# A decoder layer on one core: the last chunk's units as four heads by half the queries, and its first half's tail beside the last four units

## The chip, the cores and the metric

One core of a Trainium2 chip runs the kernel. Its engines are TensorE (PE, with a weight load of its own, PEld), VectorE (DVE), ScalarE (ACT), GpSimd (POOL) and SyncE (SP), which issues the DMAs here. Every engine works through its own queue in order and waits on semaphores. The metric is the device time of one launch in microseconds.

## The reference

Four sequences of 1024 tokens of width 256 pass a layer of three parts; each part reads the layer norm of what is so far and adds to it.

```python
h = layernorm(x)                                  # (4, 1024, 256)
q, k, v = split(h @ qkv_w.T + qkv_b)              # 16 query heads, 4 key/value heads of 64
q = q * (r / sqrt(64) * softplus(scaling))
x = x + softmax(q @ k.T) @ v @ o_w.T + o_b        # each key/value head serves 4 query heads
h = layernorm(x)                                  # cross-attention to 64 context rows, 16 heads of 16
x = x + softmax(mask(h @ Wq @ kc.T / 4)) @ vc @ Wout + bout
h = layernorm(x)                                  # routed feed-forward: 8 clusters of 8 tiles
tile = argmax over the gates of the best cluster
comp = tanh(gelu(h @ cw1) @ cw2)
mag = relu(comp @ w1[tile] + b1[tile]) @ w2[tile] + b2[tile]
x = x + layernorm(h + mag * directions[tile] * scale) * gamma + beta
```

## The kernel before

The tokens are 8 chunks of 512 (CHUNKS, two for a sequence). Attention runs in 64 units; a unit is two query heads of one key/value head over the 512 queries of a chunk, and has 8 steps (KT), one for each 128 keys. In a step PE makes the scores of both heads (`scores`: six matmuls, since q and k are kept as a high and a low part), ACT takes one exponential of 128x1024, PE multiplies the probabilities of two steps before with the values (`attend`), and DVE and POOL add them up for one head each (`add`). The maximum of each query's scores is made 11 steps ahead (`max_d`, `max_s`: two matmuls in a step, ACT's relu, DVE's row_max). `q_proj` projects a unit's queries 14 steps ahead (six matmuls of 512 columns), and ACT and DVE split them (`q_split`). Behind a unit come `raw_out`, `sums`, `inv` and `heads`, which writes the normalised outputs of two heads for 512 queries into heads_out.

What follows on attention is the tail of a chunk (`tail`): output projection and residual (`out_proj`, `x1`), norm, cross-attention in eight rounds (`scores2`, `soft2`, `exp2`, `normal2`, `weights2T`, `p2T`, `attended2`, `out2`), `projected2`, norm, routing (`route`, `compress`, `gelu`, `comp`, two calibrations `cal_a` to `cal_h`, `first_max`, `pick_tiles`, `pick_one`), the gathered weights (`pickT`, `gathered`, `spline`, `mag`, `y`), the third norm and the store.

The order of the instructions on all engines is written out by one planner, class Plan: each function is a generator that puts stages into one list and yields between them, and every engine issues its stages in the list's order. `attention` walks over the steps. In a step it first lets the lanes go on by their early part, then puts attend and add, then the late parts, then scores, then one maximum. The lane "background" holds the tail of the chunk before, beginning 5 steps behind it, so the tail of chunk 6 runs beside the units of chunk 7 (56 to 63) and is stored at 1886.08 us. All that isn't attention takes turns in two PSUM banks (ring "misc"; a stage that takes a bank waits until the one before it has been read, `freed`).

The tail of chunk 7 has no unit beside it. `last_tail` splits it in two halves of 256 queries (jobs FIRST_HALF = 7 and SECOND_HALF = 8) that take turns, the first 5 yields ahead, with seven banks. Each half has a Workspace of its own, carved from the buffers that are idle by then: the workspace of the other chunks, x_in, v_all and probs. The x of a chunk, transposed and split, lies in xT0 to xT2 (chunk modulo 3); chunk 7 uses xT1. `residual` loads x for both halves when the last sums are made, and heads_out of all eight units is needed by each half's out_proj, as every unit holds all 512 queries.

## Time and profile before

| | us |
|---|---|
| median of 3 runs (2007.4 to 2008.36) | 2007.6 |
| profiled execution | 2007.98 |
| its span, first to last instruction | 2005.0 |

| engine | busy us | share of the span | instructions |
|---|---|---|---|
| PE | 1818.2 | 91% | 9300 |
| DVE | 1153.4 | 58% | 2621 |
| ACT | 1166.0 | 58% | 1571 |
| POOL | 1010.9 | 50% | 1010 |

In forty slices of 50 us PE is busy for nine tenths in nearly all, three tenths in the first, six in the last but one and two in the last; the granted TensorE clock is 0.957 of full speed on the mean. A share over the span mixes stages with different limits: what counts for a change is the stage in which it lies, so the rows below are of the last 200 us. A matmul's duration in the timeline reaches a little into the next one, since they are pipelined; the distance of two starts is the better measure.

### The profile page before, as it was taken

The numbers are of one execution on the slowest core, as the hardware profiler recorded it, in microseconds if no ns is written. First come the engines' busy times: TensorE is split into PE (matmuls) and PEld (weight loads), VectorE is DVE, ScalarE is ACT, GpSimd is POOL, SyncE is SP. The second block draws the span as 40 slices with busy tenths as digits, with TensorE's granted clock in tenths as the row PEclk, the third lists the DMA queues.
The fourth block names the chain that finished last, engine by engine and source line by source line (L and its number), as shares of the span: only waits on it lengthen the run. The fifth ranks groups of instructions, "written<-read, shape, count | busy, mean of one in ns | idle before, by whom it ended". The sixth has DMA issues, their size and how long they took to land. (4 is left out here: it accounts for less than half of the span.)

```text
span 2005.0 us, 27355 instructions
## 1 busy us (share of the span) xinstructions
PE 1818.2 (91%) x9300; PEld 882.0 (44%) x9300; DVE 1153.4 (58%) x2621; ACT 1166.0 (58%) x1571; POOL 1010.9 (50%) x1010
## 2 busy tenths in 40 slices
PE   3999999999999989999999989989999998998962
PEld 2644454454644444453544435444464444443441
DVE  5365546556466665747457564656547556566454
ACT  3356756657466655665556665665746665666532
POOL 3344546545545554555644544564654455546633
PEclk7799999999999999999999999999999999999985
DMA  4100000000200000010200000010010000000000
GB/s 154 43 12 1 1 12 1 18 15 11 53 12 1 1 22 1 1 32 1 64 1 11 1 1 22 1 26 8 13 41 1 1 1 22 1 1 1 22 0 11
DMA packets 41307, 32.27 MB, mean 16 GB/s; under 512 B 21008, under 2 KB 35408, under 8 KB 41168
## 3 DMA queue, kind: packets, MB, share of 16 engines
q1 hardware_dynamic: 41168, 30.53, 5.8%
q8 instruction: 73, 1.20, 0.2%
q14 instruction: 66, 0.54, 0.1%
HBM read 13.48 MB, written 4.19 MB: 9 GB/s over the span
## 5 line engine op out<-in xcount | busy, mean ns | idle before, releaser
L1239 ACT ACTIVATE probs<-key_scores 128x1024 f32<-128x1024 f32 x512 | 524.2, 1024 | 532.1 <-PE key_scores L971 390.8
L1801 POOL TENSOR_TENSOR prob_sum<-prob_sum,probs 128x512 f32<-128x512 f32 x384 | 506.0, 1318 | 125.6 <-ACT probs L1239 96.9
L991 PE MATMUL attended<-probs,v_all 128*64 128x512 f32 x2048 | 566.2, 626 | 0.1
L1483 DVE CUSTOM_DVE_ANT_0 relu<-max_scores,relu 128x512 f32<-128x512 f32 x512 | 332.8, 688 | 362.2 <-PE max_scores L949 359.0
L971 PE MATMUL key_scores<-q_high,k_chain 64*128 64x512 f32 x2048 | 464.9, 450 | 39.3 <-ACT probs L1239 38.1
L971 PEld LDWEIGHTS key_scores<-q_high,k_chain 64*128 64x128 f32 x2048 | 194.8, 187 | 489.3 <-issue 242.7
L1230 ACT ACTIVATE relu<-max_scores 128x1024 f32<-128x1024 f32 x256 | 261.3, 1021 | 41.8 <-PE max_scores L949 41.7
L949 PE MATMUL max_scores<-k_max,q_high 64*128 64x512 f32 x1024 | 218.4, 422 | 49.2 <-DVE row_max L1483 42.6
L1499 DVE TENSOR_TENSOR running_sum<-running_sum,probs 128x512 f32<-128x512 f32 x320 | 221.8, 693 | 15.4 <-ACT probs L1239 6.7
L1797 POOL TENSOR_TENSOR prob_sum<-probs 128x512 f32<-128x512 f32 x64 | 84.5, 1321 | 261.5 <-PE misc L1001 256.0
L971 PE MATMUL key_scores<-q_low,k_chain 64*128 64x512 f32 x1024 | 205.6, 397 | 0.0
L991 PEld LDWEIGHTS attended<-probs,v_all 128*64 128x64 f32 x2048 | 108.0, 137 | 192.3 <-issue 189.3
L1839 POOL TENSOR_TENSOR weights<-weights,row_stat 128x512 f32<-128x512 f32 x56 | 58.4, 1042 | 199.2 <-DVE row_stat L1604 199.2
L1473 DVE SCALAR_TENSOR_TENSOR q_low<-misc,columns_sb,q_high 128x512 fp32r<-128x512 f32 x64 | 48.0, 750 | 180.8 <-ACT q_high L1221 180.8
L949 PEld LDWEIGHTS max_scores<-k_max,q_high 64*128 64x128 f32 x1024 | 99.5, 190 | 102.1 <-DVE row_max L1483 53.5
L899 PE MATMUL misc<-xT,wq_hl 128*128 128x512 f32 x384 | 111.6, 428 | 8.1 <-DVE wq_hl L1396 4.5
L1031 PE MATMUL misc<-wo,heads_out 128*128 128x256 f32 x464 | 107.8, 385 | 0.0
L971 PEld LDWEIGHTS key_scores<-q_low,k_chain 64*128 64x128 f32 x1024 | 98.9, 190 | 0.1
L1031 PEld LDWEIGHTS misc<-wo,heads_out 128*128 128x128 f32 x464 | 85.8, 190 | 22.2 <-issue 11.0
L1499 DVE TENSOR_TENSOR running_sum<-probs 128x512 f32<-128x512 f32 x64 | 91.9, 1435 | 0.9 <-ACT probs L1239 0.9
L899 PEld LDWEIGHTS misc<-xT,wq_hl 128*128 128x128 f32 x384 | 70.7, 198 | 44.9 <-issue 17.0
L1245 ACT ACTIVATE raw_out<-attended 128x512 f32<-128x512 f32 x64 | 38.2, 597 | 82.3 <-PE attended L991 82.3
(422 smaller groups left out, 2111.4 us busy)
## 6 DMA issues: line engine op xcount, KB each, us to landing
k_chain<-k_chain SPq DMA_DIRECT2D x32, 256.0 KB, 3.7
buf_a<-in_x SPq DMA_DIRECT2D x8, 512.0 KB, 4.4
k_max<-k_max SPq DMA_DIRECT2D x16, 256.0 KB, 3.7
x_in<-in_x SPq DMA_DIRECT2D x7, 512.0 KB, 4.1
out_x<-buf_b SPq DMA_DIRECT2D x7, 512.0 KB, 2.9
shift_row<-row_max SPq DMA_DIRECT2D x128, 2.0 KB, 2.0
heads_out<-in_qkv_wT SPq DMA_DIRECT2D x1, 1536.0 KB, 8.3
wo<-in_o_wT SPq DMA_DIRECT2D x1, 1024.0 KB, 6.2
```

What stands on the lines that cost most here:

```text
L899: done = tensor.matmul(ps_out, lhs(a, c), rhs(b, c), start=n == 0, stop=n == len(terms) - 1)
L949: tensor.matmul(max_scores[:, head, :], q_high[u % 3][rows, i * P:(i + 1) * P], k_max[rows, place, g // 2, first:first + 512], start=True, ...
L971: done = tensor.matmul(key_scores[:, head, :], k_chain[rows, place, part, half, keys], q[rows, :], start=kt == 0 and part == 0 and q is hi ...
L991: tensor.matmul(attended[head * HD:(head + 1) * HD, :], v_all[:, kt, g * HD:(g + 1) * HD], prob_slot(u, kt, head), start=kt == 0, stop=kt ...
L1031: done = tensor.matmul(ps[:, 0:D], heads_out[:, p, rows], wo[:, p, :], start=p == 0, stop=p == PAIRS - 1)
L1230: scalar.activation(relu[:, :, :], max_scores[:, :, :], ACT.Relu).then_inc(S["relu"])
L1239: scalar.activation(probs[(u * KT + kt) % len(probs)][:, :, :], key_scores[:, :, :], ACT.Exp).then_inc(S["exp"])
L1483: vector.tensor_tensor_reduce(out=relu[:, head, :], in0=max_scores[:, head, :], in1=relu[:, head, :], scale=1.0, scalar=-3.4e38, op0=ALU.a ...
L1499: vector.tensor_tensor(total, so_far, probabilities, ALU.add).then_inc(S["prob_sum0"])
L1797: gpsimd.tensor_tensor(prob_sum[1][:, :], prob_slot(u, 0, 1), probabilities, ALU.add).then_inc(S["prob_sum1"])
L1801: gpsimd.tensor_tensor(prob_sum[1][:, :], prob_sum[1][:, :], probabilities, ALU.add).then_inc(S["prob_sum1"])
L1839: gpsimd.tensor_tensor(w3, w3, spaces[j].row_stat[:, 2, :].unsqueeze(2).broadcast_to([P, HB, SC]), ALU.mult).then_inc(S["weights2"])
```

## The change

The last chunk's units are cut differently. Units 56 to 59 hold the first 256 queries and units 60 to 63 the second; each takes all four heads of one key/value head (two pairs, one in each half of the 512 columns). `places` lists for a unit which pair lies in which columns and which queries they are. q_proj and q_split go over these places, two in such a unit; heads writes both pairs in one instruction; out_proj of a half waits for the four units that hold its queries.

The tail of the first half begins at step 485, behind unit 59, in a lane "last" that goes on in every step, whatever the others do. What is left of it when attention ends takes turns with the second half's tail in last_tail. Its workspace is carved from x_in and from the addresses of xT0 and xT2, which chunk 7 doesn't use; the second half's comes from the rest. With that the first half's residual waits only for the projections that read these buffers, its first norm no longer for the store of chunk 6, and the second half's residual no longer for the last sums.

```diff
--- before.py
+++ after.py
@@ -72,7 +72,7 @@
 Q_AHEAD, MAX_AHEAD, SHIFT_AHEAD, PV_BEHIND, FINISH_BEHIND = 14, 11, 4, 2, 4
-HALF_AHEAD = 5
+HALF = CH // 2
 FIRST_HALF, SECOND_HALF = CHUNKS - 1, CHUNKS
@@ -87,8 +87,22 @@
-    t, p = divmod(u, PAIRS)
-    return t, p, t // PER_BATCH, p // 2
+    t, r = divmod(u, PAIRS)
+    return (t, r, t // PER_BATCH, r // 2) if t < CHUNKS - 1 else (t, None, t // PER_BATCH, r % KV)
+def last_chunk(u):
+    return u // PAIRS == CHUNKS - 1
+def places(u):
+    _, p, _, g = unit(u)
+    if not last_chunk(u):
+        return [(p, slice(0, CH), slice(0, CH))]
+    first = u % PAIRS // KV * HALF
+    return [(2 * g + n, slice(n * HALF, (n + 1) * HALF), slice(first, first + HALF)) for n in range(2)]
@@ -151,6 +165,8 @@
         return {f"max_swap{key[1]}": 16 * 2}
+    if stage == "q_split":
+        return {"q_high": len(places(key[0])), "q_low": len(places(key[0]))}
     if stage in ("residual", "store"):
@@ -499,12 +515,13 @@
         at_step((t + 1) * period + FINISH_BEHIND + 1, "background", tail, t)
+    at_step(FIRST_HALF * period + period // 2 + FINISH_BEHIND + 1, "last", tail, FIRST_HALF)
     return found
...
 def attention(plan):
-    units, preps, background = Lane(), Lane(), Lane()
-    lanes = {"preps": preps, "background": background}
+    units, preps, background, last = Lane(), Lane(), Lane(), Lane()
+    lanes = {"preps": preps, "background": background, "last": last}
     extra = work_at_steps()
@@ -525,6 +542,8 @@
             background.go_on(0, ALONE)
+        if not last.go_on(0, EARLY):
+            last.go_on(0, ALONE)
         u, kt = unit_at(-PV_BEHIND)
@@ -535,6 +554,7 @@
         background.go_on(0, LATE)
+        last.go_on(0, LATE)
         u, kt = unit_at(0)
@@ -544,20 +564,18 @@
             plan.take("max", (stage, u, i // 2), 0, (taken, (stage, u, i // 2), 0))
-        for lane in (units, preps, background):
+        for lane in (units, preps, background, last):
             lane.tidy()
-    for lane in (preps, background):
-        for generator in lane.work:
-            run(generator)
-def last_tail(plan):
+    for generator in background.work:
+        run(generator)
+    return last.work
+def last_tail(plan, begun):
     plan.holder[4], plan.holder[1] = plan.holder[3], plan.holder[0]
...
     plan.rings["misc"] = [2, 6, 7, 3, 4, 0, 1]
-    halves = [tail(plan, FIRST_HALF), tail(plan, SECOND_HALF)]
-    for _ in range(HALF_AHEAD):
-        next(halves[0])
+    halves = [tail(plan, SECOND_HALF), *begun]
     while halves:
@@ -615,8 +633,7 @@
     prologue(plan)
-    attention(plan)
-    last_tail(plan)
+    last_tail(plan, attention(plan))
@@ -685,7 +702,7 @@
         x_in = sb("x_in", [P, NT, D])
-        xT = [sb(f"xT{i}", [P, 2, KC, CH], F32R) for i in range(3)]
+        xT_last = sb("xT1", [P, 2, KC, CH], F32R)
@@ -723,12 +740,17 @@
-        regions = [flat(buffer) for buffer in (
-            main.a, main.b, main.c, main.d, main.p2T, x_in, v_all, *main.weights, *probs)]
-        def carve(name, shape):
+        with ExitStack() as until_then:
+            shared = [until_then.enter_context(nc.sbuf_tensor(f"xT{i}", [P, 2, KC, CH], F32R)) for i in (0, 2)]
+        xT = [shared[0], xT_last, shared[1]]
+        idle_x = [sb(f"idle_x{i}", [P, 2 * KC * CH]) for i in (0, 2)]
+        regions = [[flat(x_in), *(flat(buffer) for buffer in idle_x)],
+                   [flat(buffer) for buffer in (main.a, main.b, main.c, main.d, main.p2T, v_all, *main.weights, *probs)]]
+        def carve(half, name, shape):
             words = int(np.prod(shape[1:]))
-            region = min((r for r in regions if r[1] >= words), key=lambda r: r[1])
+            region = min((r for r in regions[half] if r[1] >= words), key=lambda r: r[1])
             region[1] -= words
@@ -737,7 +759,8 @@
-        halves = [Workspace(NT // 2, first, carve) for first in (0, NT // 2)]
+        halves = [Workspace(NT // 2, half * NT // 2, lambda name, shape, half=half: carve(half, name, shape))
+                  for half in range(2)]
         spaces = [main] * FIRST_HALF + halves
@@ -846,8 +869,11 @@
                     sp.wait_ge(*after("x3", "x3", j - 1, NT // 2 - 1))
+                elif j == FIRST_HALF:
+                    sp.wait_ge(*after("q_proj", "q_proj", (CHUNKS - 1) * PAIRS - 1))
+                    sp.wait_ge(*after("v_proj", "v_proj", B - 1, 1, 1))
+                    sp.wait_ge(*after("k_low", "k_low", B - 1, 1, 1))
                 else:
-                    sp.wait_ge(*after("sums", "sums", UNITS - 1))
                     sp.wait_ge(*after("store", "store", FIRST_HALF - 1))
@@ -932,13 +958,15 @@
             def q_proj(u):
-                t, p, _, _ = unit(u)
-                buf = xT[t % 3]
+                buf = xT[u // PAIRS % 3]
                 pe.wait_ge(*freed("q_proj", u))
-                pe.wait_ge(*after("xT_low", "x_split", t, KC - 1))
-                pe.wait_ge(*after("weights_low", "split_q", p // 2 > 0))
-                three_products(bank("q_proj", u)[:, :], lambda a, kc: wq_hl[:, a, kc, p * P:(p + 1) * P],
-                               lambda a, kc: buf[:, a, kc, :]).then_inc(S["q_proj"])
+                pe.wait_ge(*after("xT_low", "x_split", u // PAIRS, KC - 1))
+                for p, columns, queries in places(u):
+                    pe.wait_ge(*after("weights_low", "split_q", p // 2 > 0))
+                    done = three_products(
+                        bank("q_proj", u)[:, columns], lambda a, kc: wq_hl[:, a, kc, p * P:(p + 1) * P],
+                        lambda a, kc: buf[:, a, kc, queries])
+                done.then_inc(S["q_proj"])
@@ -1027,7 +1055,7 @@
                 for p in range(PAIRS):
-                    pe.wait_ge(*after("heads_out", "heads", t * PAIRS + p))
+                    pe.wait_ge(*after("heads_out", "heads", t * PAIRS + (p if j < FIRST_HALF else KV * (j - FIRST_HALF) + p // 2)))
                     done = tensor.matmul(ps[:, 0:D], heads_out[:, p, rows], wo[:, p, :],
@@ -1169,7 +1197,7 @@
                 act.wait_ge(*after("rstd", "stats", j, k))
-                if k == 1 and j:
+                if k == 1 and j and j != FIRST_HALF:
                     act.wait_ge(*after("store", "store", min(j, FIRST_HALF) - 1))
@@ -1214,12 +1242,12 @@
             def q_split(u):
-                _, p, _, _ = unit(u)
                 act.wait_ge(*after("q_proj", "q_proj", u))
...
                 act.wait_ge(*after("key_scores", "scores", u - 3, KT - 1))
-                scalar.activation(q_high[u % 3][:, :], bank("q_proj", u)[:, :], ACT.Identity,
-                                  bias=q_bias[:, p:p + 1]).then_inc(S["q_high"])
+                for p, columns, _ in places(u):
+                    scalar.activation(q_high[u % 3][:, columns], bank("q_proj", u)[:, columns], ACT.Identity,
+                                      bias=q_bias[:, p:p + 1]).then_inc(S["q_high"])
@@ -1468,11 +1496,11 @@
             def q_split(u):
-                _, p, _, _ = unit(u)
                 dve.wait_ge(*after("q_high", "q_split", u))
-                vector.scalar_tensor_tensor(
-                    out=q_low[u % 3][:, :], in0=bank("q_proj", u)[:, :], scalar=q_bias[:, p:p + 1],
-                    in1=q_high[u % 3][:, :].bitcast(F32), op0=ALU.add, op1=ALU.subtract).then_inc(S["q_low"])
+                for p, columns, _ in places(u):
+                    vector.scalar_tensor_tensor(
+                        out=q_low[u % 3][:, columns], in0=bank("q_proj", u)[:, columns], scalar=q_bias[:, p:p + 1],
+                        in1=q_high[u % 3][:, columns].bitcast(F32), op0=ALU.add, op1=ALU.subtract).then_inc(S["q_low"])
@@ -1802,12 +1830,14 @@
             def heads(u):
-                t, p, _, _ = unit(u)
+                taken = places(u)
+                pairs, queries = slice(taken[0][0], taken[-1][0] + 1), taken[0][2]
                 pool.wait_ge(*after("raw_out", "raw_out", u))
                 pool.wait_ge(*after("inv_sum", "inv", u))
-                pool.wait_ge(*after("out_proj", "out_proj", t - 1, NT - 1))
+                pool.wait_ge(*after("out_proj", "out_proj", u // PAIRS - 1, NT - 1))
                 pool.wait_ge(*after("weights_low", "split_v"))
-                gpsimd.tensor_tensor(heads_out[:, p, :], raw_out[:, :], inv_sum[:, :], ALU.mult).then_inc(S["heads_out"])
+                gpsimd.tensor_tensor(heads_out[:, pairs, queries], raw_out[:, :].rearrange("p (n q) -> p n q", n=len(taken)),
+                                     inv_sum[:, :].rearrange("p (n q) -> p n q", n=len(taken)), ALU.mult).then_inc(S["heads_out"])
```

## Rows read from the trace of the kernel before

**Rows 1.** Windows: length, busy PE, PEld, DVE, ACT, POOL (count), granted clock, DMA, GB/s.

```profile
1812.50:1893.90 81.40, 75.37 (x383) 31.40 (x383) 47.23 (x108) 50.76 (x68) 52.34 (x55) 0.98 0.03 7
1893.90:1926.00 32.10, 24.70 (x107) 18.24 (x106) 13.12 (x29) 8.66 (x18) 11.44 (x16) 1.00 0.06 17
1926.00:1960.00 34.00, 21.79 (x102) 12.87 (x102) 17.47 (x39) 14.57 (x28) 9.97 (x16) 0.80 0.00 0
1960.00:2005.00 45.00, 11.31 (x30) 6.16 (x28) 18.86 (x82) 9.43 (x24) 16.85 (x47) 0.51 0.04 12
```

**Rows 2.** Timeline of PE: a tail's steps; start, duration, line, operation.

```profile
1777.43 0.66 PE L1076 MATMUL misc<-consts_sb,weights 128*128 128x128 f32 x4
...
1781.21 0.64 PE L1065 MATMUL misc<-p2T,v_block 128*32 128x256 f32 x8
...
1794.41 1.99 PE L1087 MATMUL misc<-wout,buf_d 128*128 128x256 f32 x8
...
1818.40 2.00 PE L1098 MATMUL misc<-route_w,buf_c 128*128 128x72 f32 x16
...
1820.34 1.50 PE L1107 MATMUL misc<-buf_c,cw_sb 128*64 128x512 f32 x3
...
1824.09 0.95 PE L1117 MATMUL misc<-cw_sb,p2T 64*128 64x2 f32 x8
...
1893.88 3.72 PE L1031 MATMUL running_sum<-wo,heads_out 128*128 128x256 f32 x16
...
1897.43 7.07 PE L1031 MATMUL key_scores<-wo,heads_out 128*128 128x256 f32 x32
...
1909.15 1.03 PE L1046 MATMUL misc<-buf_a,wq 128*128 128x256 f32 x4
...
1913.98 1.02 PE L1055 MATMUL max_scores<-k_block,buf_a 128*128 128x512 f32 x2
```

**Rows 3.** Timeline of ACT, the exponentials of two steps of the last unit.

```profile
1885.70 1.02 ACT L1239 ACTIVATE probs<-key_scores 128x1024 f32<-128x1024 f32 x1 [1.08 <-PE key_scores L971]
1887.81 1.02 ACT L1239 ACTIVATE probs<-key_scores 128x1024 f32<-128x1024 f32 x1 [1.08 <-PE key_scores L971]
```

**Rows 4.** Timeline of PE: one value projection, one query projection.

```profile
1489.46 2.90 PE L899 MATMUL misc<-wv_hl,xT 128*128 128x128 f32 x24
...
1769.07 1.66 PE L899 MATMUL misc<-xT,wq_hl 128*128 128x512 f32 x6 [0.40 <-DVE weights L1594]
```

**Rows 5.** Timeline of PE beside the units 59 and 60, three waits and delays.

```profile
1784.69 0.66 PE L1076 MATMUL misc<-consts_sb,weights 128*128 128x128 f32 x4 [0.71 <-DVE weights L1594]
...
1812.49 0.50 PE L971 MATMUL key_scores<-q_high,k_chain 64*128 64x512 f32 x2 [1.78 <-ACT probs L1239]
...
1815.35 1.98 PE L991 MATMUL attended<-probs,v_all 128*64 128x512 f32 x4
```

**Rows 6.** Waits from 1812 to 1894: total us, times, longest.

```profile
PE max_scores L949 <- DVE row_max L1483: 2.2, 3, 1.3
```

**Rows 7.** Timeline of POOL at the end of attention.

```profile
1886.13 6.69 POOL L1801 TENSOR_TENSOR prob_sum<-prob_sum,probs 128x512 f32<-128x512 f32 x5
```

**Rows 8.** Timeline of ACT around the gelu of chunk 6.

```profile
1820.87 1.28 ACT L1316 ACT_TABLE_LOAD   x1
1822.30 0.68 ACT L1316 ACTIVATE p2T<-misc,columns_sb 64x512 f32<-64x512 f32 x1
```

**Rows 9.** Timeline of SP: the stores of the two halves.

```profile
1993.34 0.38 SPq L857 DMA_DIRECT2D out_x<-weights  x1
2002.34 0.38 SPq L857 DMA_DIRECT2D out_x<-p2T  x1
```

**Rows 10.** Timeline of DVE: first round of the first half, start and end.

```profile
1915.04 0.70 DVE L1584 TENSOR_TENSOR max_scores<-max_scores,mask_add 128x512 f32<-128x512 f32 x1 [4.51 <-PE max_scores L1055]
...
1918.60 0.20 DVE L1604 RECIPROCAL buf_c<-buf_c 128x8 f32<-128x8 f32 x1
```

**Rows 11.** Timeline of PE: projected2 of the second half.

```profile
1950.75 3.39 PE L1087 MATMUL running_sum<-wout,x_in 128*128 128x256 f32 x8
```

4 lines of the change are left out of this document (2 added, 2 removed).

## The prediction

> **How the profile was read.** First the execution's time against its span: 2007.98 us and 2005.0 us, so 2.98 us lie outside the span and I carry them over; the median of the three runs, 2007.6 us, is 0.4 us below that execution. Then the stages [rows 1]. Up to 1893.90 TensorE (PE) is busy for nearly all of the time: in the stretch from 1812.50, where the new work will be put, 75.4 of 81.4 us, so only 6.0 us are free, while DVE, ACT and POOL stand at 58%, 62% and 64%. From 1893.90 (the first output projection of the last tail) to the end, 111.1 us, PE works 57.8 us and every engine waits for another: a chain of short steps in which two half tails are interleaved. So two different things bound the kernel: PE's work ahead of 1893.90, latency behind it. Moving half a tail from the second to the first is paid at PE's price and earns latency. The question is which of the two is larger, and it is close.
>
> **What is moved, in steps.** A unit of attention is 8 steps. Counting the yields of a two-tile tail, it takes 41 steps (0 to 40). It starts at step 485 (unit 60, kt 5), and the loop ends with step 517, so steps 0 to 32 run beside attention (from the residual load to the choice of one routed tile, pick_one), and 33 to 40 (pickT, gathers, spline, y, the third norm, store) remain for last_tail. Step 485 lies at about 1812.5.
>
> **PE's price.** The steps of a tail at the full clock are in [rows 2]. A row's duration reaches into the next by 0.1 to 0.2 (3.72 us from 1893.88, and the next starts at 1897.43), so I take 0.1 off each and 0.17 off that one: two output projections of 3.55, two groups of four transposes in norm_T of 0.56, two q2 of 0.93, four scores2 of 0.92, four weights2T of 0.56 (the same four transposes), two attended2 of 0.54, one projected2 of 1.9, and half of chunk 6's route (1.9), compress (three records of four in 1.50, so 2.0) and comp (0.85). Sum 7.1 + 1.1 + 1.9 + 3.7 + 2.2 + 1.1 + 1.9 + 1.0 + 1.0 + 0.4 = 21.4 us. In the last unit a step takes 2.11 us: 1.02 of exponential and 1.08 of waiting for the next scores [rows 3]. A PE instruction put there lengthens the step by nearly all of itself, because the step's four attended matmuls, 1.08 us (a half of the 1.98 in [rows 5], which ran at half clock), already fill the time of the exponential. So no part of the 21.4 is hidden by the structure; only the 6.0 us of present gaps could take some of it.
>
> **Query projections.** The last chunk's eight become 12 products of 256 columns in place of 6 of 512. No row has 256 columns of this type. Six of 512 take 1.66 us, 24 of 128 take 2.90 us [rows 4]; 277 and 121 ns apiece. Twelve of 256 cost from 12 x 138 = 1.66 (no change, in proportion to the columns) to 12 x 173 = 2.07 us (on the line between the two), and a gain is excluded since the same columns stream. 8 x (0 to 0.4) = 0 to 3; I take 1, being nearer to the proportion to columns. The split of q in two instructions adds some 0.3 us on ScalarE (ACT) and 0.2 on VectorE (DVE) per unit; both have slack in those steps. heads keeps its 128x512 words. The order of the key groups (0 to 3 twice) changes no amount of work.
>
> **Stalls beside attention.** Three sources, each with its counterpart in the trace. (a) Two PSUM banks serve the projections, the sums, the tail of chunk 6 and now a third client. The present ring already makes PE wait, 0.71 us at 1784.69 for soft2 [rows 5]. Going through the ring: at step 486 out_proj takes the bank that norm_T of chunk 6 has just filled (about 1.1 us until it is read), at 490 norm_T takes the bank of the last q_proj, which q_low frees 1.6 us after it, at 499 to 501 four smaller ones of 0.1 to 1.1. Sum 4.9. (b) In steps 493 to 498 DVE has for two steps 8.9, 6.9 and 7.4 us of work (add 0.7, row maxima 1.4, soft2 2.1, normal2 0.9, calibration of chunk 6 up to 1.8) against PE's 5.7, 6.7 and 6.3; DVE was busy there up to nine tenths before, and PE waited for row_max 2.2 us in three places [rows 6]. Beyond PE's own increase this is 2 to 3. (c) In-order queues: norm(7,2) at step 504 holds ACT until x2 has passed mag and y of chunk 6 on DVE, and the exponential of that step is behind it: 2; norm(6,2) did the same, PE waited 1.78 us for an exponential behind it at 1812.49 [rows 5]. POOL is without a gap from 1886.13 to 1892.82 [rows 7], and beta, rstd, cal_e and cal_h (1.3 + 1.9 + 1.7 + 0.5 = 5.4 us in the last ten steps, against 2.9 us of added PE time) push it back: 2. The table loads around gelu are 1.28 us each (the first in [rows 8]); with route_ev, gelu and the two parts of inv they make 5.7 us before an exponential that PE is ready for after 4.9: 0.5. The sum of all is about 12, the upper end. The lower end is -1: POOL has 52.3 us of work in the stretch [rows 1] and gets about 14 (four normal2 of 1.04, two rstd, three pair operations, one cal_e), 64% of the longer stretch as before, a load at which PE now loses only 6.0 us, and added PE work may fill those gaps. I take +6, in the middle, since each place was found by its own row but overlapping waits count once. Attention then ends 21.4 + 1 + 6 = 28.4 us later.
>
> The first table load shows 1.28 us and gelu starts 0.15 us behind its end [rows 8]. The Trainium skill (ScalarE: Activation LUTs, What ACT_TABLE_LOAD costs) counts 2.66 us for a switch, of which 1.38 are a drain behind the load; by it two switches beside attention would take 2.8 us more than by the rows and the total would be 2014, a rule that speaks against moving a gelu there.
>
> **The tail behind attention.** Before: from 1893.90 to the second store's issue 108.4 us, and 2.7 to the end [rows 9]. After, counted from T, the end of POOL's last addition (1892.82, 1.1 us ahead of 1893.90). POOL now has pick_tiles and cal_e (0.4 and 1.7 us, the second waiting for DVE) ahead of heads(63), which ends at T+5.7, about 2 us later than it would; out_proj 0 ends at 6.6; PE waits for pick_one to 7.8, pickT, out_proj 1 to 11.7; x1, moments, rstd, norm: 16.0; norm_T and its copies 17.4; q2. ACT then has norm(7,3) of the first half ahead of q2_ev (spline after rstd, mag, y, rstd: norm from 20.4 to 21.5), so scores2 begins at T+22.4. The first half begins it now at 1913.98 = T+21.2 [rows 2]. From there the first half took 1913.98 to 1993.34 = 79.4 us with the other half in between. Alone: soft2 starts at 1915.04 and the reciprocal ends by 1918.80 [rows 10], so a round takes 3.7 us and the fourth normal2 ends after 17.1 instead of 23.8 us (6.7 less). Behind it the second half's instructions stood in front of attended2 (1.8), route (2.6), cal_exp (0.9), cal_b and cal_e (3.8), spline (2.7, behind the other's pick_one) and some smaller ones: 13 in all, by following each queue. 79.4 - 19.7 = 59.7. The store is issued at T+82.1, and 82.1 - 1.1 + 2.7 = 83.7 us follow on attention instead of 111.1.
>
> **The clock.** From 1926 to 1960 the granted clock is 0.80, behind 1960 it is 0.51 [rows 1]; in the softmax rounds it drops to half (1.2 GHz) after PE has been waiting, and comes back with the projections. A single half tail leaves PE less to do. projected2 took 1.99 at the higher level [rows 2] and 3.39 at the lower [rows 11]. Were all PE steps of the chain at the lower level, 4 to 5 us; none, 0. I take 2.5. The gain is 111.1 - 86.2 = 24.9.
>
> **Sum.** +28.4 - 24.9 = +3.5 us: 2007.98 + 3.5 = 2011.5 for such an execution, 2011 beside the median. (Less than 0.2%, 4 us, isn't to be told from no change.)
>
> **Rivals.**
> A, slower by more than 0.2%: the third client of two banks and of four in-order queues costs all that I found, 12 us, and the clock falls behind the longer waits, as at 1815.35, where an attended group took 1.98, twice its usual [rows 5], once or twice more (2 us). 21.4 + 1 + 14 - 24.9 = +11.5: 2019; it is slower from stalls of 8 on. For it: the places named. Against: most are under 2 us and can fall into the same step.
> B, faster by more than 0.2%: the added PE work fills gaps that are there anyway. Stalls -1, no cost in the projections, and the first half's remainder is out of the way sooner, so that scores2 begins at T+19: 20.4 - 24.9 - 3.4 = -7.9: 2000. For it: 65% load of the other engines. Against: these gaps come from ACT and DVE [rows 5, 6], which get more too.
> C, it doesn't do what it says: if the first half were held up (its residual comes late behind row-maximum transfers, or heads(59)), less than 33 steps would be behind it when attention ends and the two would interleave as before; What is moved and what is earned shrink together; half the move gives half of +3.5, so 2009. Little for it: the load has two steps and 4 us.
>
> **Chances.** Forecast (2005 to 2015) 0.45, A 0.29, B 0.22, C 0.04. Range 2001 to 2020: it leaves out the outer parts of A and B. Faster by over 0.2% (below 2003.6): 0.24. Within: 0.36. Slower (above 2011.6): 0.40, a good part of the forecast among it.
>
> **What would show it.** Attention's end (first out_proj of the second half) near 1922; PE's free time from 1812.5 to there near 12 us; the step of the last unit above 2.11 only where a tail instruction stands in it; heads(63) behind cal_e on POOL; q2_ev behind norm(7,3) on ACT; 86 us from there to the end; scores2 to store 60 to 63 us. The forecast is wrong if PE's free time in the stretch stays near 6 us (B), or is above 16 (A), or if the tail left is not between 80 and 90 us.

## The result and the profile after

| | before | after |
|---|---|---|
| median, us | 2007.06 (6 runs, 2001.8 to 2008.4) | 2015.11 (6 runs, 2011.8 to 2018.3) |
| ratio, 95% interval | 1 | 1.0048 (1.0031 to 1.0064), that is +9.6 us (6.2 to 12.8) |
| profiled execution, us | 2007.98 | 2014.59 |
| its span, us | 2005.0 | 2012.8 |

The change makes the kernel slower, by little. The forecast was 2011, slower by 3.5 us.

Executions of one kernel differ by up to 15 us here (the kernel before, in one set of 23 runs: 1996.2 to 2011.6), and much of that arises long before the changed place: the matmuls of step 485, up to which all kernels with the new units have one order of instructions, start anywhere from 1804.49 (e4) to 1816.88 us (e10). So the traces are laid over each other at these matmuls, which wait 1.78 us for an exponential in every kernel: 1812.49 before [rows 5], 1807.99 after. From there to the end of the span are 192.5 us before and 204.8 after. The runs below are read in the same way, in two pieces: from step 485 to the first output projection of the second half's tail (before: 81.4 us, [rows 1]), and from there to the end (before: 111.1). Windows of the kernel after, with the columns of [rows 1]; the first line answers to 1812.50:1893.90 there:

```profile
1807.99:1925.04 117.05, 104.37 (x500) 49.51 (x501) 66.31 (x165) 62.93 (x96) 65.50 (x77) 0.91 0.04 10
1925.04:1945.44 20.40, 15.26 (x53) 11.03 (x51) 6.90 (x25) 6.25 (x15) 9.76 (x22) 0.75 0.00 0
1945.44:1964.00 18.56, 10.75 (x28) 4.18 (x28) 11.69 (x20) 4.36 (x8) 5.42 (x5) 0.68 0.05 15
1964.00:2012.80 48.80, 15.04 (x46) 8.95 (x46) 11.49 (x48) 9.21 (x20) 10.77 (x29) 0.50 0.02 5
```

Beside attention 35.7 us are added (81.4 to 117.05). PE is busy 29.0 us longer and free for 12.7 us where it was for 6.0. The granted clock of the stretch went from 0.98 to 0.91. Behind attention are 87.8 us where there were 111.1, a gain of 23.3; there the clock goes 0.75, 0.68, 0.50, where it was 1.00, 0.80 and 0.51.

PE's waits and delays of the stretch, from its timeline (start, duration, line, operation, and in brackets the wait and its releaser):

```profile
1811.50 6.02 PE L1059 MATMUL misc<-wo,heads_out 128*128 128x256 f32 x16 [0.61 <-ACT buf_c L1297]
1823.39 3.72 PE L1059 MATMUL misc<-wo,heads_out 128*128 128x256 f32 x16
1838.25 0.44 PE L930 MATMUL misc<-consts_sb,x_in 128*128 128x128 f32 x2 [1.62 <-DVE q_low L1501]
1868.10 1.08 PE L1029 MATMUL misc<-prob_sum,ones 128*64 128x512 f32 x4 [1.27 <-DVE idle_x L1622]
1870.64 1.12 PE L1083 MATMUL misc<-k_block,idle_x 128*128 128x512 f32 x2 [0.77 <-ACT inv_sum L1278]
1877.29 0.84 PE L1104 MATMUL misc<-consts_sb,idle_x 128*128 128x128 f32 x4 [1.65 <-ACT buf_d L1371]
1878.06 1.97 PE L1019 MATMUL attended<-probs,v_all 128*64 128x512 f32 x4
1901.37 1.86 PE L1029 MATMUL misc<-prob_sum,ones 128*64 128x512 f32 x4 [1.82 <-ACT idle_x L1297]
1923.13 1.98 PE L1029 MATMUL misc<-prob_sum,ones 128*64 128x512 f32 x4 [2.84 <-DVE prob_sum L1527]
1925.04 5.58 PE L1059 MATMUL running_sum<-wo,heads_out 128*128 128x256 f32 x16
```

The same output projection (eight matmuls, which the trace shows as 16 records) takes 3.72 us at 1823.39 and 6.02 at 1811.50, behind the two waits of 1.78 and 0.61; attended takes 1.97 where it has 1.08, right behind the wait of 1.65, and the sums 1.86 and 1.98 instead of 1.08. So in this execution several waits are paid a second time in the half clock that follows. Not every wait is: behind the same wait of 1.78 us the clock stayed up in e2, e3, e5, e8, e9, e10 and e11 (more on this below).

Seven of these waits end when another stage has read the PSUM bank that the waiting stage takes next in the ring: 0.61 at 1811.50 (norm_ev of chunk 6), 1.62 (q_low), 1.27 (soft2), 0.77 (inv), 1.65 and a last one of 0.22 at 1882.95 (the gather of chunk 6), 1.82 (norm_ev of the first half). They make 8.0 us. The kernel before has none of them in its stretch; there PE waited 2.2 us for row maxima [rows 6] and 4.3 for exponentials, here 0.4 and 2.5.

DVE holds the last sums up: it stands in the calibration of the first half, 0.90 us waiting for POOL and 2.6 us with work of its own, before it comes to the last addition of attention (timeline of DVE). POOL isn't far ahead of it: its own last addition ends at 1922.45, DVE's at 1923.08.

```profile
1919.77 0.17 DVE L1700 TENSOR_REDUCE idle_x<-idle_x 128x2 f32<-128x16 f32 x1 [0.90 <-POOL idle_x L1894]
...
1922.40 0.68 DVE L1527 TENSOR_TENSOR prob_sum<-running_sum,probs 128x512 f32<-128x512 f32 x1
```

The steps of the tail named in the prediction, on ACT, PE and SP:

```profile
1943.48 1.09 ACT L1191 ACTIVATE x_in<-x_in,idle_x 128x256 f32<-128x256 f32 x2 [3.58 <-POOL idle_x L1792]
```

```profile
1945.44 2.05 PE L1083 MATMUL key_scores<-k_block,buf_a 128*128 128x512 f32 x2 [1.64 <-ACT buf_a L1306]
...
1967.61 3.75 PE L1115 MATMUL misc<-wout,buf_a 128*128 128x256 f32 x8 [0.59 <-ACT buf_a L1328]
```

```profile
1946.77 0.38 SPq L883 DMA_DIRECT2D out_x<-x_in  x1
2010.19 0.38 SPq L883 DMA_DIRECT2D out_x<-weights  x1
```

### The profile page after: what moved, and what is told of

It reads as the page before. It is cut to its first block and busy times, and to the rows that moved or that the text cites. A ratio compares the mean times of both kernels' runs of the same rounds, so it can differ in the third digit from the quotient of the medians.

```text
span 2012.8 us, 27467 instructions
## 1 busy us (share of the span) xinstructions
PE 1826.8 (91%) x9348; PEld 886.7 (44%) x9348; DVE 1154.4 (57%) x2629; ACT 1166.4 (58%) x1579; POOL 1011.8 (50%) x1010
## 5 line engine op out<-in xcount | busy, mean ns | idle before, releaser
L999 PE MATMUL key_scores<-q_high,k_chain 64*128 64x512 f32 x2048 | 462.8, 448 | 35.7 <-ACT probs L1267 35.2
L1501 DVE SCALAR_TENSOR_TENSOR q_low<-misc,columns_sb,q_high 128x512 fp32r<-128x512 f32 (+1 forms) x72 | 49.0, 690 | 178.2 <-ACT q_high L1249 178.2
L925 PE MATMUL misc<-xT,wq_hl 128*128 128x512 f32 (+1 forms) x432 | 109.8, 394 | 7.2 <-DVE weights L1622 3.7
L1059 PE MATMUL misc<-wo,heads_out 128*128 128x256 f32 x480 | 113.9, 391 | 0.6 <-ACT buf_c L1297 0.6
L1059 PEld LDWEIGHTS misc<-wo,heads_out 128*128 128x128 f32 x480 | 90.4, 193 | 25.0 <-issue 11.8
```

Of the source, the lines that this page charges most:

```text
L925: done = tensor.matmul(ps_out, lhs(a, c), rhs(b, c), start=n == 0, stop=n == len(terms) - 1)
L999: done = tensor.matmul(key_scores[:, head, :], k_chain[rows, place, part, half, keys], q[rows, :], start=kt == 0 and part == 0 and q is hi ...
L1059: done = tensor.matmul(ps[:, 0:D], heads_out[:, p, rows], wo[:, p, :], start=p == 0, stop=p == PAIRS - 1)
```

## The experiments

For each kernel, two windows: from step 485 to the first output projection of the (second half's) tail, and from there to the end of the span, columns as in [rows 1]. The stretches repeat closely where the clock does: the changed kernel and e4, the same up to that point, give 117.05 and 117.06.

One thing has to be kept apart from every edit. The same order of instructions shows two courses of the clock from step 485 on, in one profiled execution each. With the lane beside attention, the first output projection takes 3.72 us in e2, e3, e8, e9 and e11 (the upper course) and 6.0 to 6.1 in the changed kernel, e4 and e7 (the lower). Up to the last attended group that is 106.10 us (e2, e9) against 110.01 (the changed kernel, e4): 3.9 us that no edit made. e9 has the changed kernel's order in the whole stretch and needs 113.15 us for it, so 113.15 and 117.05 are the changed kernel's stretch on the two courses. Without the lane, the transposes and the attended group behind the wait take 1.09 and 1.08 us in e10, 1.81 and 1.98 in the kernel before (1.86 and 1.94 in e1, 1.97 and 1.18 in e12). Whether an execution or a kernel picks its course, one trace for each can't tell. An edit is judged below against the kernel on its own course.

### The units alone

```diff
-    at_step(FIRST_HALF * period + period // 2 + FINISH_BEHIND + 1, "last", tail, FIRST_HALF)
...
-    halves = [tail(plan, SECOND_HALF), *begun]
+    halves = [tail(plan, FIRST_HALF), tail(plan, SECOND_HALF)]
+    for _ in range(5):
+        next(halves[0])
```

> The changed kernel with its units cut as four heads by half the queries, but nothing beside them: both half tails run behind attention again, the first half five yields ahead. Theory (the whole cost of the change lies in the lane beside the units, none in the units' new shape): 2007 to 2009, as the kernel before, and the stretch from the scores of step 485 to the last attended group is 77 to 78 us with a granted clock of 0.98. Rival (the shape costs: twelve query projections of 256 columns instead of six of 512, four instructions of q_split instead of two, heads written across two pairs): 3 us or more above before, that is 2010 to 2012. The second half's residual and the first half's norm can start a little sooner than in the kernel before, worth at most 1 us.

Measured: 2004.5 us median against 2006.5 of the kernel before in the same runs, ratio 0.9987 (0.9973 to 1.0001).

```profile
1807.48:1890.55 83.07, 76.71 (x389) 32.36 (x389) 48.05 (x109) 50.90 (x69) 52.45 (x55) 0.96 0.05 14
1890.55:2002.30 111.75, 57.91 (x237) 38.12 (x236) 49.73 (x148) 32.63 (x70) 38.97 (x77) 0.73 0.02 5
```

The time is below the 2007 to 2009 of the theory and well below the rival's; the stretch to the last attended group is 79.0 us, a little above the 77 to 78 named. The whole stretch is 1.7 us longer than before, at a clock of 0.96 instead of 0.98; with the same units and a clock of 1.00 it is 80.2 (e10). So the shape of the units costs nothing that can be told, and the cost lies in the lane. The query projection confirms it, here of the kernel after, twelve matmuls of 256 columns in the time of six of 512 [rows 4]:

```profile
1793.95 1.69 PE L925 MATMUL misc<-xT,wq_hl 128*128 128x256 f32 x12
```

### Three of the named places taken away

The lane stands still at the end of attention:

```diff
-        if not last.go_on(0, EARLY):
+        if step < UNITS * KT and not last.go_on(0, EARLY):
...
-        last.go_on(0, LATE)
+        if step < UNITS * KT:
+            last.go_on(0, LATE)
```

> The changed kernel, but the lane with the first half's tail stands still in the last five or six steps (from step 512, when the last scores are out) and goes on when attention has ended, in turns with the second half. In the changed kernel DVE waits there for cal_h on POOL, and the last addition, the sums (2.84 us of waiting) and heads(63) stand behind it. Theory (that block of in-order queues is one of the stalls that cost more than forecast, and the moved pieces lose nothing behind attention): 3 to 4.5 us less than the changed kernel, about 2011. Rival (what is not done before attention ends is only done later, on the same queues, in front of the second half): 0 to +2 us.

More banks for the shared ring:

```diff
+        if step == UNITS * KT - MAX_AHEAD:
+            plan.holder[1] = plan.holder[0]
+            plan.rings["misc"] = [2, 6, 0, 1]
```

> The changed kernel, but from step 501, when no maximum is computed ahead any more, the two PSUM banks of the maxima join the ring of two that the projections, sums and both tails share. Theory (a third client of two banks makes PE wait: 1.82 us before the sums of unit 62, 0.22 us before an output, and the granted clock falls behind each wait, 2 us more): 2 to 4 us less than the changed kernel, about 2012. Rival (ACT or DVE is the one that is late there, the bank only passes it on, or the gap moves to the next wait): within 1 us of the changed kernel.

The second half ahead of the first behind attention:

```diff
     halves = [tail(plan, SECOND_HALF), *begun]
+    for _ in range(5):
+        next(halves[0])
```

> The changed kernel, but behind attention the second half's tail is put five yields ahead of what is left of the first half's, so that pickT of the first half no longer stands between the second half's two output projections on PE, and norm(7,3) of the first half no longer stands in front of the second half's q2_ev on ACT. Theory (these two places hold the second half's chain, as the prediction counted: scores2 at T+22.4 where its own chain would allow T+19): 3 to 4 us less than the changed kernel, about 2011.5. Rival (the softmax rounds are bound by something else, or the first half's remainder now collides with the rounds): 0 to 1 us less.

Measured: 2019.1 us (ratio 1.0058, 1.0036 to 1.0080), 2015.7 (1.0051, 1.0033 to 1.0068) and 2015.8 (1.0046, 1.0030 to 1.0063), against 1.0048 (1.0031 to 1.0064) of the change: none is better. Windows of e2, e3 and e4:

```profile
1816.58:1928.20 111.62, 99.78 (x501) 46.97 (x501) 64.78 (x158) 62.71 (x95) 65.23 (x76) 0.97 0.04 10
1928.20:2019.80 91.60, 40.58 (x125) 23.13 (x124) 31.95 (x99) 20.17 (x44) 26.35 (x56) 0.64 0.02 6
```

```profile
1811.25:1924.20 112.95, 97.73 (x501) 45.73 (x501) 68.55 (x162) 63.16 (x96) 65.54 (x77) 0.98 0.04 10
1924.20:2012.80 88.60, 38.27 (x126) 22.53 (x124) 30.78 (x96) 19.85 (x43) 25.94 (x55) 0.64 0.02 6
```

```profile
1804.49:1921.55 117.06, 104.34 (x500) 49.45 (x500) 66.33 (x165) 62.94 (x96) 65.59 (x77) 0.91 0.04 10
1921.55:2009.60 88.05, 40.23 (x126) 24.13 (x124) 29.94 (x93) 19.97 (x43) 25.96 (x55) 0.62 0.02 6
```

e2: the last part of attention, from the last attended group to the first output projection, fell from 7.0 to 5.5 us, and 3.8 us came back behind attention (91.6 against 87.8). The rival held: the pieces are only done later. Its first window is shorter than the changed kernel's by 5.4 us, but 3.9 of them are the upper course of the clock; 1.5 are the edit's. The sums now wait 1.37 us for POOL's last addition, the next one behind DVE's.

e3: the 1.82 us ahead of the sums of unit 62 went, but the row maxima now hold the bank of a gather, and the wait for norm_ev (L1300 here, L1297 in the kernel after) came back one stage on. Timeline of PE in e3:

```profile
1882.88 1.49 PE L1166 MATMUL max_scores<-table,p2T 64*128 64x322 f32 x4 [1.51 <-DVE row_max L1514]
...
1904.48 1.08 PE L1129 MATMUL max_scores<-route_w,idle_x 128*128 128x72 f32 x8 [1.17 <-ACT idle_x L1300]
```

Up to the last attended group e3 needs 106.70, against 106.10 for e2 and e9 on the same course: nothing is won, as the rival said. The releaser had said it: that wait ended with ACT's norm_ev, of which the bank was only the carrier. The two banks join from step 501 on, so e3 says nothing of the five bank waits before that, 5.9 us together; more banks for those no run tried.

e4 gained nothing, neither the 3 to 4 us of its theory nor the up to 1 us of the rival: 88.0 us behind attention against 87.8. scores2 of the second half begins at T+22.3 where the changed kernel has T+22.4 (T is now the end of DVE's last addition, 1919.60 and 1923.08, which ends later than POOL's). pickT and norm(7,3) are out of the way, and the first half's gather at half clock stands between norm_T and q2 in their place:

```profile
1934.74 0.65 PE L932 MATMUL max_scores<-consts_sb,weights 128*128 128x128 f32 x4 [3.92 <-ACT weights L1193]
1935.33 2.26 PE L1165 MATMUL misc<-table,idle_x 64*128 64x322 f32 x4
1937.52 2.07 PE L1076 MATMUL running_sum<-buf_a,wq 128*128 128x256 f32 x4
```

### Less of PE's work

```diff
-                for p in range(PAIRS):
+                for p in range(PAIRS) if j != FIRST_HALF else (PAIRS - 1,):
...
-                                         start=p == 0, stop=p == PAIRS - 1)
+                                         start=p == 0 or j == FIRST_HALF, stop=p == PAIRS - 1)
```

> The changed kernel, but each of the first half's two output projections makes only one of its eight products per matmul group (this leaves out most of that half's attention output): 14 of 16 matmuls of 256 columns less on PE beside the units, 6.2 of 7.1 us at the full clock. The waits of the other engines, the order of all stages and the banks stay. Theory (beside attention every us of PE work is paid in full, and a part again in the granted clock): the stretch from the scores of step 485 to the last attended group is 6 to 9 us shorter than 110.0. Rival (the stretch is held by ACT, DVE and POOL, PE's work fills their gaps): 0 to 3 us shorter. The tail behind attention stays at 87 to 88 us under both.

The kernel leaves out seven of eight products of the first half's output projections, so its numbers are only good for its time. Measured: 2006.8 us, ratio 1.0010 (0.9995 to 1.0025).

```profile
1809.99:1914.96 104.97, 90.41 (x473) 40.10 (x473) 67.32 (x164) 62.80 (x96) 65.64 (x77) 0.99 0.04 11
1914.96:2002.00 87.04, 38.58 (x126) 22.96 (x124) 30.20 (x94) 19.73 (x43) 25.95 (x55) 0.64 0.02 6
```

Up to the last attended group it needs 97.40 us. That is 12.6 less than the changed kernel's 110.01, but e5 runs on the upper course (it waits 1.29 us ahead of its first output projection, as e2 does), and against the 106.10 of that course it is 8.7 less for 6.2 us of work: the theory's 6 to 9. So this work is paid in full and 2.5 us more, in clock. PE's free time did not shrink by the added work: 14.6 us here, 13.3 in e9, 12.7 in the changed kernel. The rival's 0 to 3 us are out.

Against the kernel before, PE is busy 15.0 us longer; with the 6.2 left out that is 21.2, near the 21.4 of the prediction, and the rest of the changed kernel's +29.0 is clock, 7.8 us. The kernel before has some half clock of its own in the stretch, though. Against e10, at 1.00, PE is busy 16.7 us longer in e5, which gives 22.9 us for the lane's work and leaves 6.1 for what the changed kernel loses to the clock beyond the kernel before. So the work lies between 21.2 and 22.9 and the clock between 6.1 and 7.8.

### How much to move

The lane stands still from a step on (504 here, 494 in the second), and goes on behind attention:

```diff
-        if not last.go_on(0, EARLY):
+        if step < 504 and not last.go_on(0, EARLY):
...
-        last.go_on(0, LATE)
+        if step < 504:
+            last.go_on(0, LATE)
```

> The changed kernel, but the first half's lane stands still from step 504 on (behind projected2 and x2); norm_T, route, compress, gelu, comp and the calibrations of the first half then take turns with the second half behind attention. Known so far: standing still from step 512 on takes 1.5 us out of the wait ahead of the sums and adds 3.8 us behind attention. Theory (beside attention the late pieces cost PE's price of 3.0 us and stalls of 5 us and more, behind it they hide beside the second half's chain except for places in a queue): the stretch from the scores of step 485 to the first output projection of the second half is 7 to 10 us shorter than the changed kernel's 117, the rest 4 to 7 us longer than 87.8; in all 1 to 5 us less, about 2012. Rival (behind attention they cost as much as they did in the kernel before, 24 us for 41 steps, so some 12 for 20): the total is 2 to 5 us above the changed kernel's.

> The changed kernel, but the first half's lane stands still from step 494 on, behind its output projections, first norm and q2: PE gets 9.6 us of the 21.4 beside attention. Theory (price beside attention is PE's work plus stalls that go with the number of pieces): the stretch from the scores of step 485 to the first output projection of the second half is 16 to 20 us shorter than 117, so 97 to 101. Behind attention both halves' softmax rounds run side by side again, which took 6.7 us more than one half alone by the prediction's reading, and the first half's later pieces stand in the second's way (13 us by that reading), less what its head start spares: 12 to 18 us longer than 87.8. In all 0 to 6 us less than the changed kernel, 2009 to 2015. Rival (what counts behind attention is only the second half's own chain, and a first half that is ten steps ahead no longer stands in its way): the rest is 3 to 8 us longer and the total 10 us less, 2003 to 2005.

(The numbers of steps there are one too high: 9 and 19 run beside attention, the 9 with one scores2, 10.5 us of PE's work.) Measured: 2014.1 us (ratio 1.0048, 1.0031 to 1.0065) and 2008.3 (1.0011, 0.9995 to 1.0028). Windows of e7 and e8:

```profile
1812.76:1920.45 107.69, 98.21 (x481) 45.85 (x481) 62.65 (x140) 57.81 (x85) 60.39 (x65) 0.95 0.04 11
1920.45:2016.10 95.65, 44.15 (x145) 25.93 (x144) 34.95 (x117) 25.20 (x54) 30.87 (x67) 0.66 0.02 6
```

```profile
1809.11:1900.95 91.84, 84.94 (x435) 38.89 (x435) 51.90 (x118) 53.03 (x75) 56.22 (x61) 1.00 0.04 12
1900.95:2004.10 103.15, 53.90 (x191) 32.41 (x190) 48.01 (x139) 30.39 (x64) 35.11 (x71) 0.64 0.02 6
```

e7 (lower course) went as its theory, but for the part behind attention, 7.9 us longer instead of 4 to 7. e8's stretch is 25.2 us shorter than the changed kernel's, and 21.3 shorter than e9's on its own, the upper course; the theory had 16 to 20. The rest is 15.4 longer, as the theory had it.

The prices of the pieces, on like courses: the first nine steps cost 11.6 us beside attention (e10's 80.22 to 91.84) and earn 8.6 behind it (111.75 to 103.15). Laid over e1, which ran on the lower course, they would seem to cost only 8.8 and to break even, but the ratios of the runs speak for the loss: 1.0011 against 0.9987, 4.8 us, though the intervals overlap a little. The next ten cost about 12 (15.9 between e8 and e7, less the 3.9 between the courses, an estimate) and earn 7.5; the last fourteen cost 9.4 (e7 to the changed kernel, both lower) and earn 7.9. So no part of the move pays by itself. The first nine steps are nearly all PE work, 11.2 of 11.6 us; the later ones bring waits with them. Behind attention the clock is 0.73 with the whole tail there (e1), 0.64 (e8) and 0.66 (e7) with less of it, and 0.60 to 0.64 with the changed kernel's share (0.60 there, 0.62 in e4, 0.64 in e5).

### Holding the clock

```diff
+            fillers = {
+                ("norm_T", 8, 1, 0): 5, ("scores2", 8, 0): 3, ("weights2T", 8, 0): 6, ("weights2T", 8, 1): 1,
...
+            def filler(n):
+                pe.wait_ge(*after("raw_out", "raw_out", UNITS - 1))
+                for i in range(n):
+                    tensor.matmul(attended[:, 0:D], ident, wo[:, i % PAIRS, :], start=True, stop=True)
             for stage, *key in plan.entries:
                 if stage in stages:
+                    filler(fillers[stage, *key]) if (stage, *key) in fillers else None
                     stages[stage](*key)
```

In the trace each of these matmuls shows as two records. e10 and e12 have this on the kernel of the units alone, e11 on the lane that stops at 494, each with a table fitted to its own gaps.

> The changed kernel, but in the second half's tail behind attention PE multiplies constants (wo by the identity, 256 columns, into the bank of attended, read by nobody) in the gaps in which it waited: 5 such matmuls ahead of norm_T, 3 ahead of scores2, 6, 1, 1 and 6 ahead of the four weights2T, 9 ahead of the third norm_T, 28 ahead of pickT, one in four smaller gaps. At 0.35 to 0.45 us each at the lower clock they fit the gaps seen. Theory (the granted clock of 0.50 to 0.75 behind attention comes from PE's waiting, and costs 5 us on the chain: q2 0.9, scores2 1.0, projected2 1.7, route and compress 1.4): the clock there rises towards 1.00 and the tail takes 82 to 84 us instead of 87.8. Rival 1 (the clock isn't held by such work): 88 to 90 us, as some of the filling delays the chain. Rival 2 (the clock rises, but the chain is bound by other engines): 87 to 88 us.

> The units of four heads by half the queries with both half tails behind attention (as in the run that only has the units), and PE's gaps there filled in the same way with multiplications of constants. Theory (the clock behind attention, 0.73, is PE's waiting, and most of PE's steps there stand on the chain of one half or the other): 4 to 6 us less than that run, so about 107 us behind attention instead of 111.8 and 1999 to 2001 in all, faster than both kernels. Rival (filling delays one half or the other as often as it quickens a step, or doesn't hold the clock): 111 to 114 us, 2004 to 2007.

> The changed kernel with the first half's lane standing still from step 494 on (ten steps of its tail beside attention, 9.6 us of PE's work), and PE's gaps behind attention filled with multiplications of constants. It asks whether a small move pays once the clock behind attention is held. Theory (a step moved beside attention costs its PE work in full and gives back less behind it, whatever the clock): the stretch from the scores of step 485 to the first output projection is 91.8 as without filling, the rest 97 to 99 instead of 103.2, together 189 to 191, above the 187.2 of the filled kernel with nothing beside attention. Rival (the clock was what kept the move from paying): the rest is 92 to 95 us, together 184 to 187.

> The filled kernel with both half tails behind attention once more, its filling fitted to what its trace showed: ahead of pickT of the first half 30 instead of 20 multiplications (PE waited 3.06 us there after 20, and its gather then took 2.51 us at half clock), ahead of pickT of the second 4 instead of 5, none ahead of the gather, one more in two of the larger gaps. Theory (more of the chain at the full clock): 105 to 107 us behind attention instead of 107.0, 2002 to 2004 in all, and below the kernel before by more than the interval. Rival (the filling that remained too long for its gap costs what the clock gives): 107 to 109 us, 2004 to 2006.

Measured, each against the kernel before in its runs: e9 2012.3 us (ratio 1.0024, 1.0010 to 1.0039), e10 2004.1 (0.9983, 0.9967 to 0.9999), e11 1998.9 (0.9977, 0.9961 to 0.9992), e12 2002.1 (0.9995, 0.9979 to 1.0011). Windows of e9, e10, e11, e12, and of e9 the same steps as above (transposes, q2 and scores2 from PE's timeline):

```profile
1809.94:1923.09 113.15, 99.82 (x501) 47.33 (x501) 66.82 (x165) 62.95 (x96) 65.68 (x77) 0.96 0.04 10
1923.09:2004.30 81.21, 58.25 (x252) 41.69 (x250) 29.95 (x93) 19.63 (x43) 26.05 (x55) 0.88 0.02 7
```

```profile
1816.88:1897.10 80.22, 73.75 (x388) 31.14 (x388) 47.01 (x109) 50.92 (x69) 52.58 (x55) 1.00 0.05 14
1897.10:2004.10 107.00, 76.17 (x347) 54.64 (x346) 49.59 (x148) 32.56 (x70) 39.06 (x77) 0.88 0.02 6
```

```profile
1815.22:1906.76 91.54, 84.95 (x434) 38.88 (x434) 50.68 (x118) 53.06 (x75) 56.36 (x61) 1.00 0.04 12
1906.76:1998.50 91.74, 70.00 (x325) 50.43 (x324) 47.87 (x139) 30.24 (x64) 35.26 (x71) 0.90 0.02 7
```

```profile
1815.34:1897.07 81.73, 75.27 (x388) 32.16 (x388) 47.02 (x109) 50.93 (x69) 52.58 (x55) 0.98 0.05 14
1897.07:2004.10 107.03, 77.02 (x371) 56.60 (x370) 49.62 (x148) 32.66 (x70) 39.07 (x77) 0.92 0.02 6
```

```profile
1933.82 2.43 PE L1182 MATMUL attended<-wo,consts_sb 128*128 128x256 f32 x10
1936.77 0.66 PE L930 MATMUL misc<-consts_sb,weights 128*128 128x128 f32 x4 [0.52 <-ACT weights L1202]
1938.04 1.10 PE L1074 MATMUL running_sum<-buf_a,wq 128*128 128x256 f32 x4 [0.62 <-ACT buf_a L1308]
1938.98 1.03 PE L1074 MATMUL key_scores<-buf_a,wq 128*128 128x256 f32 x4
...
1963.30 1.97 PE L1115 MATMUL misc<-wout,buf_a 128*128 128x256 f32 x8
```

The five filling matmuls ahead of norm_T took 2.43 us, 0.49 each, a little more than the 0.35 to 0.45 expected.

e9: the clock behind attention is 0.88, two q2 groups take 1.10 and 1.03 us where they took 2.04 and 1.91 at the lower clock, projected2 1.97 instead of 3.75, and the tail 81.2 instead of 87.8. So the lower clock cost the changed kernel 6.6 us there. All of it lies behind scores2, which begins 20.4 us after the first output projection in both. e10: 107.0 us behind attention instead of 111.8, as its theory said; but the time, 2004.1 us, falls into the rival's 2004 to 2007, and beside the ratio of e1 (0.9983 and 0.9987) the runs show no gain from this filling. e12 holds the clock better than e10 (0.92) and needs 107.03, so its fuller filling brought nothing more; against its theory its ratio shows no difference from the kernel before.

e11 is the surprise: its theory fell, and it went slightly beyond its rival (92 to 95, together 184 to 187). With nine steps moved and the clock held, the part behind attention takes 91.7 us, 11.4 less than without filling and 15.3 less than e10's, while the move costs 11.3 beside attention (80.22 to 91.54). Laid over at step 485 it needs 183.3 us, against 192.5 of the kernel before, 187.2 of e10 and 188.8 of e12; the changed kernel with filling needs 194.4. In the medians of the same runs it is 5.3 us below the kernel before, by the ratio 4.6 (1.6 to 7.8); the traces, which leave out the first 1810 us, give 9.2, and that difference stays open. Of all kernels only e11 and e10 have intervals below 1, and e10's ends at 0.9999. That filling helps on one and the same order is shown by the ratios for e8 and e11 (1.0011 and 0.9977, with intervals that don't meet); for the changed kernel and e9 the intervals overlap. That e11 beats e10 rests on the laid-over traces, not on the ratios, whose intervals overlap too.

## Why the prediction came out as it did

The direction and the range held; the sum was too low, by 4 us beside the median and by 6 beside the ratio, and the median of 2015.1 lies at the very edge of the forecast's 2005 to 2015. Two of its terms failed, both in the clock, and two others came out near their size by errors that offset each other.

- PE's price, 21.4: right within 1.5. e5 gives 21.2 beside the kernel before and 22.9 beside e10. "No part is hidden" held too: rival B asked for PE's free time near 6 us; it was 12.7.
- Query projections, 1 (0 to 3): 0.2. A projection takes 1.69 us instead of 1.66, near the lower bound of the two.
- Stalls beside attention, +6: right in size, in part by luck. PE is free for 12.7 us instead of 6.0, +6.7; the forecast named "near 12". The banks were the largest source in the forecast, 4.9, and cost more: 8.0, of which 6.1 stand at the places named (486, 490, 499 to 501; q_low with 1.62 for the 1.6 forecast) and 1.8 at a place that was not, step 507. The wait ahead of the last sums, 2.84 us, was not placed rightly either: POOL at the end was counted with 2 us and its own queue blamed, and what holds the sums is DVE's calibration, with POOL's last addition 0.6 us behind it. Against these stand waits that became shorter and that the forecast had growing: for row maxima 0.4 us instead of 2.2 (source b: 2 to 3 more), for exponentials 2.5 instead of 4.3 (source c: 2 more). The gelu's loads cost nothing that the trace shows: the exponential behind them waited 0.73 us for PE, not PE for it.
- The step that failed first: the clock beside attention. The sum had no term for it there; only rival A had one, "once or twice more (2 us)". It cost 6.1 to 7.8 us in the profiled execution: 35.7 = 21.2 work + 7.8 clock + 6.7 waits, where the forecast had 28.4. Attention's end, named near 1922, lies at 1929.5 on the kernel before's time line. Some 3.9 us of it are the course of the clock; which of the two an execution takes the forecast couldn't know. On like courses the kernels laid over each other differ by 12.3 us (both on the lower) and 9.6 (both on the upper: e9's stretch against e10's, with the parts behind attention as they were); the ratio gives 9.6.
- The tail behind attention, 86.2 with the clock: 87.8. heads(63) at T+5.4 (T+5.7 predicted), out_proj 1 ends at T+11.4 (11.7), norm at T+15.6 (16.0), norm(7,3) from T+20.4 to 21.5 (the same), scores2 at T+22.4 (the same), scores2 to the store's issue 64.7 (59.7 and 2.5 for the clock; "60 to 63"). The total is near by luck, since two errors offset each other: the clock cost 6.6 (e9) and not 2.5, and the rest of the chain is shorter than counted by some 2.5: 81.2 with filling instead of 83.7, and 58.2 from scores2 to the store's issue instead of 59.7.
- e4 shows the limit of such a count. It was right about who stood in front of scores2, and still there was no gain: with these gone, the next in the queue stood there.
- The Trainium skill's rule on table loads (ScalarE: Activation LUTs, What ACT_TABLE_LOAD costs) would have made two switches 2.8 us dearer than the rows. The trace sides with the rows, on either side of the load. In e8, timeline of ACT, the load starts 0.02 us behind the end of the gelu, and an exponential starts 0.01 us behind the end of the load. That the 2014 us by that rule lie nearer to the measured 2015 than the forecast's 2011 is chance:

```profile
1945.13 0.47 ACT L1345 ACTIVATE idle_x<-max_scores,columns_sb 64x256 f32<-64x256 f32 x1 [0.31 <-PE max_scores L1136]
1945.62 1.28 ACT L1185 ACT_TABLE_LOAD   x1
1946.91 0.63 ACT L1313 ACTIVATE buf_b<-buf_b 128x512 f32<-128x512 f32 x1
```

- Rival A (slower, stalls of 8 on and clock) has the mechanism that the runs show for what the forecast missed. Its 14 us (12 of stalls, 2 of clock) were 14.5 in the profiled execution, at a different split: 6.7 and 7.8. Its +11.5 is near the +12.3 of the traces; the forecast and A share the 9.6 of the runs between them.

## What to carry to other kernels

Where an engine's clock falls behind its waits, as TensorE's did here, a move has two prices that a sum of durations leaves out: waits put into a busy stretch can be paid again in the matmuls behind them, and the stretch that the work leaves may be emptier and slower. So judge such a move with the clock held too: without filling, nine moved steps lost 3 us, with it they gained 4 us more than the filling alone, both by the laid-over traces. Before calling a difference of two traces the work of an edit, look for a place where both have the same instructions at different clocks: 2.9 to 3.9 us were that here, enough to make a loss look even. And a short stall removed from four in-order queues that are full mostly turned into the next one here (e2, e3, e4), so ask for the one behind it before counting its time as gained.

## What the runs showed of the hardware

- The granted clock can be held by matmuls that nobody reads. Multiplications of constants in PE's gaps took the clock behind attention from about 0.6 to 0.88 (the changed kernel to e9) and from 0.64 to 0.90 (e8 to e11), and the stretches became 6.6 and 11.4 us shorter. The same projected2 (eight records) took 1.97 and 3.75 us at the two levels (2.4 and 1.2 GHz), an output projection (16 records) 3.72 and 6.02, the latter in part at either level.
- The same instruction order gives two courses of the clock: 106.10 us (e2, e9) and 110.01 (after, e4) up to the last attended group, both behind the same wait of 1.78 us. In the second the transposes behind it took 1.77 us and not 1.09, so PE waited 0.61 us ahead of the output projection and not 1.29. What decides between them no run here shows.
- Matmuls of 256 columns in this type cost in proportion: 141 ns each, against 277 for 512 and 121 for 128 [rows 4]. For the same columns in all, 256 at a time costs what 512 does; 128 at a time (the value projection) costs 1.7 times as much a column.
